# Dense products with no reader ahead of two waits of TensorE

## The chip, the cores and the metric

The kernel runs on one core of a Trainium2 chip. The metric is the device time of one execution in microseconds (us), lower is better. A run with the hardware profiler switched on gives the trace from which the rows below come.

## The reference, cut to what matters

2 x 2048 token ids out of 64 become rows of 256 numbers: 179 from an embedding table, 77 from a projected magnitude spectrum of the one-hot signal, interpolated between 33 frames. Then

```
h = tok(x)                                            # (2, 2048, 256)
h = h + local_attention(layernorm(h))                 # softmax over 5 neighbours
h = h + moe(layernorm(h))                             # 8 experts, top 2, capacity 1280
# moe: logits = x @ router_w + b; two best experts of each token, weights renormalised
#      h1 = gelu(rows of an expert @ w1[e] + b1[e]);  out = h1 @ w2[e] + b2[e]
```

## The kernel before, in words

A token's row is a mixture of 98 table rows (64 ids, 33 frames, one constant). The attention stage works on 8 groups (`NG`) of 512 tokens, each of 4 tiles of 128. All its products are of 32-bit operands. The order is written out by hand for each engine, with semaphores between the engines.

TensorE's order for one group is `attend(g)`: `mix(g)` (lines 1192 and 1194, probabilities times table coordinates), `scores(g + 1)` (line 1164, then transpositions at 1169 and 1171), `residual(g)` (lines 1205 and 1206, two products for each tile), `turn_probs(g + 1)` (lines 1182 and 1183: it waits for the probabilities and transposes them), `table_times_u(g + 2)` (line 1157), and `rank(c)` where a chunk of groups has been routed (lines 1218 to 1225). `turn_probs` waits for `probs_ready` from VectorE, and for `hc_ready`, ScalarE's copies of all four tiles of `residual`. Inside `residual` tile t waits for ScalarE's copy of tile t - 2.

ScalarE copies the score coordinates (533), the transposed tables (539), the exponentials (548), the turned probabilities (554), the mixture (589), the residual's results (600), and scales rows for the experts (567) and for the output (576). Its exponentials of group g + 1 stand between the copies of `residual(g)`. VectorE adds the mask to the scores (794), takes the maximum (798), normalises (804, 806), takes statistics (818), and runs the routing of a chunk as chains of small instructions (842 to 958), after which it makes the low halves of the rows (966). The chunks of routing are groups 0 and 1, 2 and 3, 4 and 5, 6, 7.

GpSimd sends the routed rows to device memory, one indirect DMA for each tile and each of the two choices (451). When the first choices of all chunks have been sent (`sent_low`), SyncE's queue loads the rows of the first half expert, transposed (421), and their meta data (423). TensorE then runs `layer1` (1261) and `layer2` (1275) on 16 half experts, products of 16-bit operands with 320 and 256 columns. GpSimd adds the results to the output by indirect DMA (474).

`bank[0]` holds scores of two of a group's four tiles until VectorE has added the mask (`masked`); `w1s[:, 0, 0, 0, :]` is written when the first weight pair has been made (`stage_free`).

Of the kernel before, what the change touches and what calls it, by code (L numbers as in the profile page):

```python
# [33 lines left out]
P = 128  # L34
# [32 lines left out]
CHUNKS = ((0, 2), (2, 2), (4, 2), (6, 1), (7, 1))  # L67
# [23 lines left out]
def wait(eng, sem, value):  # L91

    if isinstance(value, int) and value <= 0:
        return
    eng.wait_ge(sem, value)


def build(nc, ids_frames, ids_win, window, emb, proj_w, proj_b, wq, wk, wv, bqk, bv, wr, br,
          w1, b1, w2, b2, consts, frames_of, masks, out):
    with ExitStack() as ctx:  # L100
        def sb(name, shape, dt=F32):
            return ctx.enter_context(nc.sbuf_tensor(name, shape, dt))

        def sem(name):
            return ctx.enter_context(nc.semaphore(name))


        w1s = sb("w1s", [P, 2, E, 2, FF], F16)
# [97 lines left out]
        def route(dims, dt=F32):  # L206
# [40 lines left out]
        bank = [ctx.enter_context(nc.psum_tensor(f"bank{i}", [P, 512], F32)) for i in range(8)]  # L247
# [30 lines left out]
        u_ready, g_done, g_ready, s_done, masked, max_ready, nmax_ready = (sem(n) for n in (  # L278
            "u_ready", "g_done", "g_ready", "s_done", "masked", "max_ready", "nmax_ready"))
# [5 lines left out]
        hout_ready, scaled, pair_hi, stage_free = (sem(n) for n in (  # L285
            "hout_ready", "scaled", "pair_hi", "stage_free"))
# [10 lines left out]
        sent_low = [sem(f"sent_low{c}") for c in range(len(CHUNKS))]  # L297
# [9 lines left out]
        def chunk_tiles(c):  # L307
            first, n = CHUNKS[c]
            return range(TPG * first, TPG * (first + n))
# [742 lines left out]
        def _(pe):  # L1052
            mm = nc.tensor.matmul
# [27 lines left out]
            for b in range(B):  # L1081
                for kt in range(2):
                    last = mm(bank[5][0:KZ, b * KZ:(b + 1) * KZ], tcT[:, kt, b, :], tcT[:, kt, b, :],
                              start=(kt == 0), stop=(kt == 1))
# [23 lines left out]
            for b in range(B):  # L1108
                for kt in range(2):
                    mm(bank[5][0:KZ, b * H:(b + 1) * H], tcT[:, kt, b, :], wv_s[:, kt, :],  # L1110
                       start=(kt == 0), stop=False)
                last = mm(bank[5][0:KZ, b * H:(b + 1) * H], con[0:1, C_ROW97:C_ROW97 + KZ], bv_s[0:1, :],
                          start=False, stop=True)
# [4 lines left out]
            for b in range(B):  # L1118
                for j in range(2):
                    last = mm(bank[4][0:KZ, b * KZ:(b + 1) * KZ], qT[:, j, b, :], kT[:, j, b, :],  # L1120
                              start=(j == 0), stop=(j == 1))
# [23 lines left out]
            for n, src in enumerate((tcT, tvT)):  # L1145
                for b in range(B):
                    at_ = (n * B + b) * E
                    for kt in range(2):
                        last = mm(bank[3][0:KZ, at_:at_ + E], src[:, kt, b, :], wr_s[:, kt, :],
                                  start=(kt == 0), stop=(kt == 1))  # L1150
# [8 lines left out]
            def scores(g):  # L1159
# [8 lines left out]
                for t in range(TPG):  # L1168
# [2 lines left out]
                nc.tensor.transpose(bank[5][0:2 * WCTX, TPG * KZ:(TPG + 1) * KZ], u[:, GRP:WIN],  # L1171
                                    ident[0:KZ, 0:KZ]).then_inc(ut_done, 1)

            def turn_probs(g):

                pe.wait_ge(probs_ready, g + 1)
                if g == 0:
                    pe.wait_ge(tabs_ready, 2)
                wait(pe, prT_ready, 2 * g)
                wait(pe, hc_ready, TPG * g)  # L1180
                for t in range(TPG):
                    nc.tensor.transpose(bank[3][:, t * P:(t + 1) * P], pr[:, t, 0:P], ident)  # L1182
                    last = nc.tensor.transpose(bank[7][0:2 * WCTX, EXTRA + t * 32:EXTRA + (t + 1) * 32],
                                               pr[P - 32:P, t, P:KEYS], ident[P - 32:P, P - 32:P])
                last.then_inc(pt_done, 1)
# [23 lines left out]
            def rank(c):  # L1209

                tiles = chunk_tiles(c)
                n = len(tiles)
                first, groups = CHUNKS[c]
                pe.wait_ge(counts_ready, c + 1)
                pe.wait_ge(misc_ready, 5)
                pe.wait_ge(ut_ready, 2 * min(first + groups + 2, NG))
                cells = counts[:, tiles[0]:tiles[-1] + 1, :]
                mm(ranks[:, 0:n * E], tri_b[:, :], cells.rearrange("p t e -> p (t e)"), start=True, stop=False)
                if c:
                    mm(ranks[:, 0:n * E].rearrange("p (t e) -> p t e", e=E), ones_b[:, :],  # L1220
                       before_b[:, :].unsqueeze(1).to_broadcast([P, n, E]), start=False, stop=False)
                for t in range(n - 1):
                    mm(ranks[:, (t + 1) * E:n * E].rearrange("p (t e) -> p t e", e=E), ones_b[:, :],
                       cells[:, t:t + 1, :].to_broadcast([P, n - 1 - t, E]), start=False, stop=False)
                mm(ranks[:, 0:n * E].rearrange("p (t e) -> p t e", e=E), ones_b[0:1, :],
                   base_b[0:1, :].unsqueeze(1).to_broadcast([1, n, E]), start=False, stop=True).then_inc(ranks_done, 1)

            def attend(g):
                more, more2 = g + 1 < NG, g + 2 < NG
                mix(g)  # L1230
                if more:
                    for c in ended(g - 2):
                        pe.wait_ge(ranks_read, c + 1)
                    scores(g + 1)
                residual(g)
                if more:
                    turn_probs(g + 1)
                if more2:
                    table_times_u(g + 2)
                for c in ended(g - 1):  # L1240
                    rank(c)

            table_times_u(0)
            scores(0)
            turn_probs(0)
            table_times_u(1)
            for g in range(NG):
                attend(g)
            rank(len(CHUNKS) - 1)


            def layer1(k):
# [125 lines left out]
```

## Time and profile before

| | |
|---|---|
| three runs | 472.61 us median (471.72 to 472.97) |
| the profiled execution | 467.62 us |
| its span, first to last instruction | 465.6 us |
| mean granted TensorE clock | 0.859 |
| TensorE busy | 364.2 us (78%) |
| VectorE, ScalarE, GpSimd busy | 273.2, 219.0, 227.2 us |

The clock is given as a share of full speed: 1.00 is 2.4 GHz, 0.50 is 1.2 GHz, and a mean between them is a stretch that had both. PE is TensorE, PEld its loading of the stationary operand, DVE VectorE, ACT ScalarE, POOL GpSimd, SPq SyncE's queue. Attention runs from about 62 to 198 us, the hand-over to the experts from 198 to 238 us, the experts from 238 us on.

### The profile page before, as it was taken

The numbers are of one execution on the slowest core, as the hardware profiler recorded it, in microseconds if no ns is written. First come the engines' busy times: TensorE is split into PE (matmuls) and PEld (weight loads), VectorE is DVE, ScalarE is ACT, GpSimd is POOL, SyncE is SP. The second block draws the span as 40 slices with busy tenths as digits, with TensorE's granted clock in tenths as the row PEclk, the third lists the DMA queues.
The fourth block names the chain that finished last, engine by engine and source line by source line (L and its number), as shares of the span: only waits on it lengthen the run. The fifth ranks groups of instructions, "written<-read, shape, count | busy, mean of one in ns | idle before, by whom it ended". The sixth has DMA issues, their size and how long they took to land.

```text
span 465.6 us, 7030 instructions
## 1 busy us (share of the span) xinstructions
PE 364.2 (78%) x2541; PEld 274.3 (59%) x2541; DVE 273.2 (59%) x753; ACT 219.0 (47%) x472; POOL 227.2 (49%) x167
## 2 busy tenths in 40 slices
PE   3079966998995995900059999999999999999950
PEld 3067443766762763600037778888877778888740
DVE  5824663448548458875009766666777766666630
ACT  3217876565562563541036554444555554444520
POOL 1035753300345346447740666555565676646682
PEclk9999975799596597565569999999999999999995
DMA  7839719866324223253288687778877787735463
GB/s 187 214 99 377 251 37 384 369 255 223 94 91 134 81 82 122 89 182 115 101 196 153 79 109 112 104 106 107 103 113 81 95 106 108 109 40 56 55 68 34
DMA packets 83462, 63.10 MB, mean 136 GB/s; under 512 B 56176, under 2 KB 77041, under 8 KB 82050
## 3 DMA queue, kind: packets, MB, share of 16 engines
q1 hardware_dynamic: 68836, 43.25, 34.1%
q0 software_dynamic: 14592, 19.41, 25.7%
q8 instruction: 20, 0.33, 0.3%
q14 instruction: 14, 0.11, 0.1%
HBM read 16.09 MB, written 36.06 MB: 112 GB/s over the span
## 4 chain that ended last, share of the span: by engine, by line
PE 61%; DVE 12%; POOL 9%; issue 6%; DMA 6%; ACT 2%; SPq 1%; ACTq 0%; DVEq 0%; POOLq 0%
PE bank L1261 20%; PE bank L1275 17%; POOL out L474 6%; PE bank L1192 3%; POOL slot_rows L451 3%; PE bank L1157 3%; PE bank L1205 3%; PE bank L1194 2%; PE bank L1182 2%; PE bank L1206 2%; DMA out<-reg_h,meta 2%; PE bank L1164 2%; DMA con<-consts 2%; PE bank L1069 1%; ACT reg_a L548 1%
## 5 line engine op out<-in xcount | busy, mean ns | idle before, releaser
L474 POOL DMA_INDIRECT out<-reg_h,meta x80 | 128.0, 1600 | 90.1 <-DVE reg_h L1038 57.8
L1261 PE MATMUL bank<-reg_z,w1s 128*128 128x320 f16 x768 | 108.8, 303 | 26.0 <-DMA meta<-slot_rows 26.0
L1275 PE MATMUL bank<-w2s,reg_h 128*128 128x256 f16 x960 | 107.3, 273 | 2.0 <-DVE reg_h L1030 2.0
L1261 PEld LDWEIGHTS bank<-reg_z,w1s 128*128 128x128 f16 x768 | 75.7, 99 | 55.9 <-issue 26.1
L451 POOL DMA_INDIRECT slot_rows<-reg_z,slots x64 | 64.2, 1003 | 89.5 <-DVE reg_z L966 73.0
L1275 PEld LDWEIGHTS bank<-w2s,reg_h 128*128 128x128 f16 x960 | 93.7, 98 | 14.1 <-DVE reg_h L1030 2.3
L641 ACT ACTIVATE reg_a<-bank,b1s 128x320 f32<-128x320 f32 x128 | 67.4, 527 | 37.4 <-PE bank L1261 33.1
L1038 DVE SCALAR_TENSOR_TENSOR reg_h<-reg_p,meta,reg_h 128x256 f32<-128x256 f32 x80 | 38.8, 485 | 55.8 <-ACT reg_h L653 49.3
L653 ACT ACTIVATE reg_h<-bank,meta 128x256 f32<-128x256 f32 x80 | 37.9, 474 | 68.2 <-PE bank L1275 64.9
L1028 DVE TENSOR_SCALAR reg_h<-reg_a 128x320 f16<-128x320 f32 x128 | 49.9, 390 | 33.5 <-DMA slot_rows<-reg_z,slots 27.1
L1030 DVE SCALAR_TENSOR_TENSOR reg_h<-reg_a,reg_h 128x320 f16<-128x320 f32 x128 | 63.0, 492 | 4.4
L1205 PE MATMUL bank<-ta,reg_a 98*128 98x265 f32 x64 | 25.7, 491 | 8.2 <-issue 6.0
L1206 PE MATMUL bank<-tb,reg_a 98*128 98x265 f32 x64 | 24.0, 464 | 0.0
L438 POOL TENSOR_TENSOR w1s<-reg_h,w1s 128x1024 f16<-128x1024 f32 x6 | 12.8, 2130 | 21.6 <-ACT w1s L492 21.6
L1205 PEld LDWEIGHTS bank<-ta,reg_a 98*128 98x128 f32 x64 | 14.0, 241 | 13.2 <-issue 7.3
L1182 PE MATMUL bank<-con,reg_a 128*128 128x128 f32 x32 | 12.3, 386 | 10.9 <-DVE reg_a L806 9.2
L794 DVE TENSOR_TENSOR reg_a<-bank,reg_a 128x264 f32<-128x264 f32 x16 | 6.2, 427 | 22.6 <-PE bank L1164 22.6
L1192 PE MATMUL bank<-reg_a 128*98 128x128 f32 x64 | 19.1, 390 | 0.4 <-ACT reg_a L555 0.4
L966 DVE SCALAR_TENSOR_TENSOR reg_z<-reg_h,r,reg_z 128x256 f16<-128x256 f32 x32 | 13.6, 480 | 8.4 <-ACT reg_z L567 8.2
L600 ACT ACTIVATE reg_h<-bank 128x265 f32<-128x265 f32 x32 | 12.3, 383 | 12.1 <-PE bank L1206 7.2
L1206 PEld LDWEIGHTS bank<-tb,reg_a 98*128 98x128 f32 x64 | 15.1, 236 | 3.7
L1069 PE MATMUL bank<-reg_a,reg_h 128*33 128x77 f32 (+1 forms) x68 | 6.7, 270 | 13.1 <-DVE reg_h L714 13.1
(167 smaller groups left out, 426.5 us busy)
## 6 DMA issues: line engine op xcount, KB each, us to landing
slot_rows<-reg_z SPq DMA_DIRECT2D x8, 1360.0 KB, 9.5
reg_h<-w SPq DMA_DIRECT2D x12, 512.0 KB, 8.6
out<-reg_p SPq DMA_DIRECT2D x8, 512.0 KB
reg_w<-w SPq DMA_DIRECT2D x4, 512.0 KB, 10.2
reg_a<-inv_rows SPq DMA_DIRECT2D x8, 193.5 KB
out<-reg_z SPq DMA_DIRECT2D x1, 1280.0 KB, 13.0
out<-reg_h,meta POOLq DMA_INDIRECT x80
reg_a<-masks SPq DMA_DIRECT2D x1, 1056.0 KB, 12.9
```

The source lines that it names most:

```text
L451: nc.gpsimd.indirect_dma_start(out=slot_rows, out_offset=bass.IndirectOffsetOnAxis(ap=slots[:, side, n:n + 1], axis=0), in_=x2w[:, n % RIN ...
L474: nc.gpsimd.indirect_dma_start(out=out.rearrange("t p c -> (t p) c"), out_offset=bass.IndirectOffsetOnAxis(ap=meta[:, k, s, 0:1], axis=0), ...
L641: nc.scalar.activation(gel[:, n % GB, :], bank[n % 4][:, 0:CH], ACT.Gelu, bias=b1s[:, e, f:f + 1], scale=1.0 / (X_SCALE * W_SCALE)).then_i ...
L653: nc.scalar.activation(y[:, k % 2, s, :], bank[4 + n % 4][:, 0:H], ACT.Copy, scale=metaf[:, k, s, 1 + e:2 + e]).then_inc(y_scaled, 1)
L1028: ts(hT[:, k % 2, 0, f, cols], gel[:, n % GB, :], X_SCALE, None, ALU.mult).then_inc(hi_ready, 1)
L1030: stt(hT[:, k % 2, 1, f, cols], gel[:, n % GB, :], X_SCALE, hT[:, k % 2, 0, f, cols], ALU.mult, ALU.subtract).then_inc(lo_ready, 1)
L1038: stt(y[:, k % 2, s, :], b2s[:, e, :], metaf[:, k, s, 1 + e:2 + e], y[:, k % 2, s, :], ALU.mult, ALU.add).then_inc(y_ready, 1)
L1192: mm(bank[2][0:KZ, t * P:(t + 1) * P], ut[:, t, :], prT[:, t * P:(t + 1) * P], start=True, stop=False)
L1205: mm(bank[6 + t % 2][:, 0:OW], zq[:, t * P:(t + 1) * P], ta_b, start=True, stop=False)
L1206: mm(bank[6 + t % 2][:, 0:OW], yT[:, t * P:(t + 1) * P], tb_b, start=False, stop=True).then_inc(o_done, 1)
L1261: last = mm(bank[n % 4][:, 0:CH], w1s[:, wp, e, kt, f * P:(f + 1) * P], xT[:, k % XB, 2 * xp + kt, c * CH:(c + 1) * CH], start=(kt == 0 an ...
L1275: last = mm(bank[4 + n % 4][:, 0:H], hT[:, k % 2, hp, f, s * P:(s + 1) * P], w2s[:, wp, e, f, :], start=(f == 0 and hp == 0 and wp == 0), ...
```

## The change: what it does

A helper `keep_busy(n)` issues n products of 128x128 by 128x512 16-bit operands, weights in both places, into `bank[0]`. Each starts its own sum and nobody reads the bank before it is written again. Four of them stand in `turn_probs(g)` ahead of the wait for probabilities, for g from 1 to 7; they wait until group g's scores have been read out of the bank, and for the weights. Twelve stand between the last `rank` and the first `layer1`, behind a wait for the last chunk's first-choice rows, the event that also lets SyncE load the first half expert.

```diff
+            def keep_busy(n):
+
+                for i in range(n):
+                    mm(bank[0][:, :], w1s[:, 0, 0, 0, 0:P], w1s[:, 0, 0, 0, :], start=True, stop=True)
+
             def turn_probs(g):
 
+                if g:
+                    pe.wait_ge(masked, 2 * (g + 1))
+                    pe.wait_ge(stage_free, 1)
+                    keep_busy(4)
                 pe.wait_ge(probs_ready, g + 1)
...
             rank(len(CHUNKS) - 1)
+            pe.wait_ge(sent_low[len(CHUNKS) - 1], 16 * len(chunk_tiles(len(CHUNKS) - 1)))
+            keep_busy(12)
```

## Rows read from the trace of the kernel before

**Rows 1.** The span in 40 slices: TensorE's busy tenths and granted clock.

```profile
PE   3079966998995995900059999999999999999950
PEclk9999975799596597565569999999999999999995
```

**Rows 2.** The chain that ended last, shares of the span by engine.

```profile
PE 61%; DVE 12%; POOL 9%; issue 6%; DMA 6%; ACT 2%; SPq 1%; ACTq 0%; DVEq 0%; POOLq 0%
```

**Rows 3.** Busy time, clock (the 0.5 to 1.0), DMA: turning to turning, groups 1 to 7.

```profile
91.17:102.15 10.98, 10.41 (x55) 7.28 (x56) 4.74 (x14) 7.14 (x22) 0.00 (x0) 1.00 0.52 184
102.15:114.49 12.34, 10.49 (x55) 7.29 (x55) 11.06 (x50) 7.28 (x23) 0.00 (x0) 1.00 0.82 299
114.49:131.85 17.36, 16.79 (x64) 11.91 (x65) 8.85 (x28) 9.52 (x28) 4.18 (x4) 0.61 0.23 74
131.85:149.83 17.98, 12.31 (x56) 7.84 (x56) 12.61 (x54) 7.96 (x25) 11.62 (x12) 0.81 0.41 135
149.83:166.88 17.05, 16.48 (x66) 11.43 (x66) 8.62 (x28) 9.41 (x28) 4.16 (x4) 0.60 0.18 63
166.88:183.26 16.38, 11.80 (x55) 7.73 (x56) 12.42 (x53) 7.96 (x25) 11.15 (x12) 0.91 0.35 125
183.26:198.50 15.24, 14.19 (x56) 9.97 (x56) 11.42 (x56) 6.80 (x18) 5.69 (x6) 0.53 0.23 83
```

**Rows 4.** The same view of two stretches at the low clock.

```profile
115.70:129.20 13.50, 13.50 (x51) 9.76 (x51) 6.55 (x22) 7.70 (x21) 4.18 (x4) 0.50 0.30 96
181.00:197.30 16.30, 14.68 (x51) 9.78 (x51) 13.58 (x65) 7.28 (x20) 6.37 (x7) 0.50 0.23 84
```

**Rows 5.** TensorE in order of time: start, length, and in brackets the idle before.

```profile
97.68 0.64 PE L1205 MATMUL bank<-ta,reg_a 98*128 98x265 f32 x2
...
102.15 0.32 PE L1182 MATMUL bank<-con,reg_a 128*128 128x128 f32 x1 [0.57 <-DVE reg_a L806]
...
114.49 0.33 PE L1182 MATMUL bank<-con,reg_a 128*128 128x128 f32 x1 [1.85 <-DVE reg_a L806]
...
142.36 0.81 PE L1205 MATMUL bank<-ta,reg_a 98*128 98x265 f32 x2 [2.03 <-issue]
...
145.51 1.25 PE L1205 MATMUL bank<-ta,reg_a 98*128 98x265 f32 x2 [1.45 <-ACT reg_h L600]
...
149.83 0.47 PE L1182 MATMUL bank<-con,reg_a 128*128 128x128 f32 x1 [2.19 <-DVE reg_a L806]
...
180.56 1.25 PE L1205 MATMUL bank<-ta,reg_a 98*128 98x265 f32 x2 [1.98 <-issue]
...
183.26 0.45 PE L1182 MATMUL bank<-con,reg_a 128*128 128x128 f32 x1 [0.57 <-issue]
```

**Rows 6.** ScalarE in order of time, in rounds 3 and 7.

```profile
118.75 2.49 ACT L567 ACTIVATE reg_z<-reg_h,r 128x256 f16<-128x256 f32 x6
121.14 1.69 ACT L576 ACTIVATE reg_p<-reg_h 128x256 f32<-128x256 f32 x4
...
193.15 0.23 ACT L583 ACTIVATE reg_r<-reg_r 128x32 f32<-128x32 f32 x1 [1.45 <-DVE reg_r L883]
```

**Rows 7.** VectorE in order of time, in rounds 4 and 7.

```profile
142.55 0.77 DVE L794 TENSOR_TENSOR reg_a<-bank,reg_a 128x264 f32<-128x264 f32 x2
...
199.26 0.88 DVE L966 SCALAR_TENSOR_TENSOR reg_z<-reg_h,r,reg_z 128x256 f16<-128x256 f32 x2 [2.21 <-ACT reg_z L567]
```

**Rows 8.** GpSimd in order of time, behind the attention stage.

```profile
207.61 1.35 POOL L451 DMA_INDIRECT slot_rows<-reg_z,slots  x1 [5.35 <-DVE reg_z L966]
```

**Rows 9.** The chain in order of time, at the first experts: start, length, what.

```profile
227.98 2.46 DMA slot_rows<-reg_z,slots
...
233.56 3.89 DMA meta<-slot_rows
237.58 15.27 PE bank L1261 x96
...
259.40 6.52 PE bank L1261 x48
```

## The prediction

> **What bounds the kernel now.** I read the span in slices first [rows 1]: from slice 21 on TensorE is busy without a break at full clock, so the experts stay as they are; the granted clock is down in the attention slices and around the hand-over. The chain of waits puts 61% on TensorE [rows 2]. The question is thus where TensorE works at the low clock while it sets the pace. For that I cut attention at the start of each turning of probabilities, rounds 1 to 7 [rows 3]. Rounds 1 and 2 run at 1.00 and take 10.98 and 12.34 us. Rounds 3 and 5 run at 0.61 and 0.60, with TensorE busy 16.8 of 17.4 and 16.5 of 17.1 us: TensorE sets the pace there, slowly. Rounds 4 and 6 have it busy for 12.3 of 18.0 and 11.8 of 16.4 us; another engine rules. In round 4 VectorE adds the mask at 142.55 us with no idle time before it, so it is late from its own routing chain, and TensorE's breaks of 2.03, 1.45 and 2.19 us follow from that [rows 5, 7]. Round 7 is at 0.53, and in it TensorE works 14.2 of 15.2 us.
>
> The low stretch of round 3 is 13.5 us at 0.50 (1.2 GHz), with no break in the work [rows 4]. Just before it TensorE sat idle for 1.85 us ahead of the third turning [rows 5]. The falls in rounds 4 and 6 come with breaks of about 2 us inside `residual`; no filler stands there. In both the clock was low again when the next odd round began.
>
> **What leads from attention to the end.** Behind attention GpSimd sat idle for 5.35 us until 207.61 us, then sent rows without a stop [rows 8]; it started when VectorE had the rows, which hangs on the last residual copies. So what round 7's end gains or loses goes through to the experts, up to those 5.35 us for a gain that VectorE's or GpSimd's own work does not share.
>
> **One filler's price.** The trace has no 512-column product. 48 products of 320 columns take 6.52 us at full clock, 0.136 us each or 0.424 ns a column [rows 9]: 512 columns take 0.217 us, four 0.87 us. In the first 96, which took 15.27 us, 2.23 us went to the low clock against 13.04. At half the clock a product costs twice: four take 1.74 us, twelve 5.2 us. Bounds: if their issue were as slow as two instructions of the turning (0.32 us one by one at full clock, [rows 5]), four would take 1.3 us; if the engine takes them while it would wait anyway, nothing. I take 0.87 and 1.74.
>
> **Where four fillers cost.** A turning starts 0.57 us after the residual's last product, even where the probabilities are there, since it waits for ScalarE's last copy. That is so in the rows of turnings 2 and 7 and three more times [rows 5]. There, warm fillers cost 0.87 - 0.57 = 0.3 us: turnings 1, 2, 4 and 6, 1.2 us. At turning 7 the clock is low (1.2 GHz from 181 us, [rows 4]), so 1.74 - 0.57 = 1.15 us (bounds 0.3 and 1.2). Ahead of turnings 3 and 5 TensorE waits 1.85 and 2.19 us [rows 5]; fillers of 0.87 and 1.74 fit in: nothing. The added waits for `masked` and the weights are long past there: masked scores are what the exponentials are made from. Sum of costs 2.35 us.
>
> **Round 3, the gain.** With 0.87 us of dense products in it the 1.85 us break becomes 0.98 us, less than half of the breaks at which the clock fell. I take it that the clock stays at full here. What is the round then worth? Round 1 took 10.98 us, all warm. Round 3 has two things more: a `rank`, and on ScalarE six scalings of rows and four output copies, 4.08 us from 118.75 to 122.83, ahead of the copy of the mixture [rows 6]. In round 1 the residual started 97.68 - 91.17 = 6.5 us after the turning [rows 5]. In a warm round 3, ScalarE would be through the coordinates' copy some 3.1 us after the turning, with its 4.08 us at 7.2 and with the mixture (0.6 us) at about 7.75: the residual starts 1.2 us later than in round 1. That covers the rank, too. 10.98 + 1.2 = 12.2 us against 17.36 us [rows 3]: a gain of 5.2 us (bounds: 0 if the clock falls all the same; 6.4 if ScalarE's copies cost nothing). The next round starts as much earlier, and all of its order with it, VectorE's routing included, since that starts from this round's copies.
>
> **Rounds 4 to 7.** Round 4 keeps its length of 18 us, bound by VectorE; its breaks inside `residual` have no filler, so I expect the clock low at turning 5 as before, round 5 the same as now, and round 6 and 7 the same but for the costs above.
>
> **The twelve.** They may start when the last chunk's first rows are down, about 230.4 us (227.98 + 2.46), and the first half expert's rows land at 237.5 us [rows 9]. Twelve at the low clock take 5.2 us and end at 235.6, ahead of the landing: no cost. If the clock rises on the way they end sooner. Either way about 2 us of idle time follow, as long as the breaks at which the clock fell in attention [rows 5]. So of the 2.23 us at most I take 1.0 us (bounds 0 and 2.2).
>
> **Sum.** + 2.35 - 5.2 - 1.0 = - 3.85 us. The profiled execution of before is 467.62 us (span 465.6), which gives 463.8. The timed runs have a median of 472.61, 5.0 us above the profiled one, so the forecast for them is 468.8 us.
>
> The moment at which the clock turns is the weak point. Worked out of the mean clocks, rounds 3, 5 and 7 spent 13.5, 13.6 and 14.3 us at the low one (twice the missing share by the length, [rows 3]), and in each it rose only near the round's end. The Trainium skill ("TensorE: Matmul & The Clock Gate", Part 1, section "What's actually happening") says that the number of products run cold at a start varies between runs of one kernel. By that rule the 5.2 and 1.0 us are not a property of the kernel alone, and the before of another execution might not fall at turning 3; one profiled execution can't show it.
>
> **Rivals.**
> - The fillers also lift the clock ahead of turning 5 or 7. There the residual's last tile is followed by 1.74 us of dense work, in all 3.9 us with hardly a break from 145.51 or 180.56 us [rows 5]. For it: the clock has risen in `residual` before, the densest stretch. Against: it took many us of work each time. At turning 5 a warm round would be some 12.2 us long, as worked out above, against 17.05: 4.8 us more gained. At turning 7 VectorE's routing limits it: ScalarE waits until 193.15 us for VectorE's logits [rows 6], and only the residual's tail shortens; since VectorE's rows at 199.26 us have 2.21 us of idle time in front [rows 7], 2.2 us is all that can be given, and the 1.15 us cost goes too: 3.35 us. Times: 464.0 (turning 5), 465.4 (turning 7), 460.6 (both).
> - Slower: the clock falls in round 3 all the same. Place: turning 3. 0.98 us of idle time are left there, and the turning waits on its transpositions behind it; that is enough for the fall. Price: the costs stand, 2.35 us, the gain is 0, and where the twelve bring nothing either (they end 2 us early) the time is 475.0 us. It decides if the granted clock is 0.5 within 2 us of turning 3.
> - The timed runs of before do not have the fall of round 3, as in the rule above: nothing to save there, - 3.85 + 5.2 = + 1.35, 474.0 us. Against it: their times lie within 1.25 us, less than 5.2, so they'd have to share another pattern; and they are slower than the profiled one, not faster.
> - Round 3's gain is given back: VectorE, GpSimd's sending or the transfers hold round 4 at its old place. Half of the gain gone makes 471.4 us. Against it: VectorE idles 2.6 us more than once in round 3, busy 8.85 of 17.36 us [rows 3].
>
> **How the numbers follow.** Forecast 0.30; further rises 0.36 (only at 7 0.17, only at 5 0.12, both 0.07); falls all the same 0.17; before without the fall 0.07; given back 0.10. Two runs of this kernel can be told apart from about 0.3%, 1.4 us. Faster by more: the forecast and the rises and 0.06 of the rest, 0.72. Slower by more: most of the fourth and some of the fifth case, 0.15. Same: 0.13. The range leaves out the double rise and most of the slower case with no help from the twelve: 461.0 to 474.5 us.
>
> **What would show it.** In the changed trace: the clock at 1.00 from turning 3 to the break in round 4's residual, and round 3 about 12 us long (right), or 17 (wrong). Fillers of 0.217 us each warm, 0.43 cold. Turnings 1, 2, 4, 6 0.3 us later behind the residual. Round 4 still 18 us, round 5 at 0.6. A first half expert of 13 to 15.3 us. The prediction is wrong if round 3 keeps its length, if round 4 grows by what round 3 gave, or if the clock is at 1.00 in round 5 or 7.

## The result, and the profile after

The changed kernel takes 466.75 us (median of 4 runs, 464.33 to 467.81) against 472.17 us before (4 runs, 471.15 to 472.97): a ratio of 0.9879, 95% interval 0.9835 to 0.9924, some 5.4 us faster. The forecast was 468.8 us in a range of 461.0 to 474.5. The profiled execution took 464.33 us with a span of 462.5 us and a mean clock of 0.876 (before: 467.62, 465.6 and 0.859). Where a kernel had a run more than 1.5% above its fastest, that run is not in its ratio; this is one run each of three kernels below (468.74, 534.70 and 471.95 us).

The same cut as in [rows 3], turning to turning, for the changed kernel; after the busy times come clock, DMA share and GB/s. The last two rows are the hand-over and the first 96 expert products:

```profile
91.24:102.32 11.08, 11.08 (x60) 7.68 (x59) 4.74 (x13) 7.14 (x22) 0.00 (x0) 1.00 0.53 191
102.32:114.61 12.29, 11.31 (x60) 7.55 (x59) 10.95 (x50) 7.28 (x23) 0.00 (x0) 1.00 0.81 296
114.61:126.92 12.31, 11.70 (x69) 8.26 (x69) 8.76 (x28) 9.18 (x28) 4.19 (x4) 1.00 0.28 84
126.92:146.43 19.51, 13.46 (x61) 8.18 (x59) 12.73 (x54) 8.08 (x25) 11.66 (x12) 0.82 0.38 137
146.43:163.54 17.11, 17.11 (x69) 11.87 (x70) 8.75 (x28) 9.41 (x28) 4.17 (x4) 0.61 0.19 64
163.54:181.41 17.87, 13.46 (x61) 8.21 (x60) 12.94 (x55) 7.96 (x25) 11.66 (x12) 0.87 0.34 124
181.41:195.90 14.49, 13.55 (x56) 9.45 (x56) 10.91 (x54) 6.93 (x18) 5.68 (x6) 0.57 0.23 81
195.90:234.80 38.90, 5.01 (x19) 1.88 (x20) 15.38 (x68) 6.02 (x16) 25.70 (x26) 0.56 0.47 150
234.80:249.67 14.87, 14.87 (x98) 10.24 (x99) 9.12 (x26) 8.97 (x16) 1.36 (x2) 0.89 0.83 156
```

The third row is the gain: round 3 went from 17.36 us at 0.61 to 12.31 us at 1.00. Rows 4 and 6 give part of it back: 19.51 for 17.98 us and 17.87 for 16.38 us. Together that is 3.0 us of the 5.05. Round 5 is as it was, round 7 is 0.9 us shorter (turning to the start of the last `rank` in both traces, 14.09 for 14.98 us) and the first 96 products 0.4 us.

TensorE in order of time, changed kernel, around turnings 3, 5 and 7 and at the hand-over (L1177 are the fillers, L1191 the turning):

```profile
112.60 1.03 PE L1177 MATMUL bank<-w1s 128*128 128x512 f16 x4
114.61 0.33 PE L1191 MATMUL bank<-con,reg_a 128*128 128x128 f32 x1 [0.99 <-DVE reg_a L806]
...
142.48 1.91 PE L1177 MATMUL bank<-w1s 128*128 128x512 f16 x4
146.43 0.47 PE L1191 MATMUL bank<-con,reg_a 128*128 128x128 f32 x1 [2.04 <-DVE reg_a L806]
...
179.11 1.91 PE L1177 MATMUL bank<-w1s 128*128 128x512 f16 x4
181.41 0.45 PE L1191 MATMUL bank<-con,reg_a 128*128 128x128 f32 x1 [0.38 <-ACT reg_h L600]
...
227.79 4.58 PE L1177 MATMUL bank<-w1s 128*128 128x512 f16 x12 [18.98 <-DMA slot_rows<-reg_z,slots]
234.80 14.87 PE L1272 MATMUL bank<-reg_z,w1s 128*128 128x320 f16 x96 [2.43 <-issue]
```

The idle time ahead of turning 3 went from 1.85 to 0.99 us [rows 5] and the clock stayed. Ahead of turning 5 it is still 2.04 us, behind fillers of 1.91 us. That is what is odd in the trace: round 4 had a wait of 2.19 us for them to fit in [rows 5], and should not have grown. ScalarE shows why, in round 4 of the changed kernel:

```profile
140.13 0.37 ACT L600 ACTIVATE reg_h<-bank 128x265 f32<-128x265 f32 x1
142.13 0.39 ACT L600 ACTIVATE reg_h<-bank 128x265 f32<-128x265 f32 x1 [0.86 <-remote]
145.71 0.39 ACT L600 ACTIVATE reg_h<-bank 128x265 f32<-128x265 f32 x1 [3.18 <-remote]
```

The residual's last tile was done at 142.7 us and its copy starts 3.0 us later, with no releaser that the profile knows ("remote"). I call this a hold-up below. The experiments had to say whether the fillers cause it.

### The profile page after: what moved, and what is told of

Read it like the earlier page. It is cut to its first block, busy times and chain, and to the rows that moved or that the text cites. A ratio compares the mean times of both kernels' runs of the same rounds, so it can differ in the third digit from the quotient of the medians.

```text
span 462.5 us, 7117 instructions
## 1 busy us (share of the span) xinstructions
PE 368.0 (80%) x2581; PEld 274.0 (59%) x2581; DVE 273.7 (59%) x753; ACT 218.6 (47%) x472; POOL 227.1 (49%) x167
## 4 chain that ended last, share of the span: by engine, by line
PE 61%; DVE 16%; POOL 8%; issue 6%; DMA 4%; ACT 3%; another core or an unknown queue 1%; SPq 0%; DVEq 0%; ACTq 0%; POOLq 0%
PE bank L1272 22%; PE bank L1286 19%; POOL out L474 4%; POOL slot_rows L451 3%; PE bank L1157 2%; PE bank L1214 2%; PE bank L1164 2%; PE bank L1191 2%; PE bank L1177 2%; PE bank L1201 2%; DMA con<-consts 2%; PE bank L1215 2%; PE bank L1069 1%; DVE reg_z L966 1%; PE bank L1203 1%
## 5 line engine op out<-in xcount | busy, mean ns | idle before, releaser
L1214 PE MATMUL bank<-ta,reg_a 98*128 98x265 f32 x64 | 24.3, 467 | 9.3 <-issue 6.0
L1177 PE MATMUL bank<-w1s 128*128 128x512 f16 x40 | 13.5, 484 | 19.0 <-DMA slot_rows<-reg_z,slots 19.0
L438 POOL TENSOR_TENSOR w1s<-reg_h,w1s 128x1024 f16<-128x1024 f32 x6 | 12.8, 2130 | 21.5 <-ACT w1s L492 21.5
L1215 PE MATMUL bank<-tb,reg_a 98*128 98x265 f32 x64 | 22.2, 433 | 0.0
L1214 PEld LDWEIGHTS bank<-ta,reg_a 98*128 98x128 f32 x64 | 12.9, 224 | 14.0 <-issue 7.3
L1177 PEld LDWEIGHTS bank<-w1s 128*128 128x128 f16 x40 | 4.7, 120 | 25.5 <-DMA slot_rows<-reg_z,slots 19.1
L600 ACT ACTIVATE reg_h<-bank 128x265 f32<-128x265 f32 x32 | 12.3, 383 | 15.8 <-remote 6.7
L1201 PE MATMUL bank<-reg_a 128*98 128x128 f32 x64 | 17.9, 369 | 0.2 <-ACT reg_a L555 0.2
L1191 PE MATMUL bank<-con,reg_a 128*128 128x128 f32 x32 | 12.0, 376 | 7.4 <-DVE reg_a L806 7.0
```

The source lines that it names most:

```text
L1177: mm(bank[0][:, :], w1s[:, 0, 0, 0, 0:P], w1s[:, 0, 0, 0, :], start=True, stop=True)
L1214: mm(bank[6 + t % 2][:, 0:OW], zq[:, t * P:(t + 1) * P], ta_b, start=True, stop=False)
L1215: mm(bank[6 + t % 2][:, 0:OW], yT[:, t * P:(t + 1) * P], tb_b, start=False, stop=True).then_inc(o_done, 1)
```

## The experiments

All ran in groups, each group on one chip with its own runs of the kernel before: 467.0 us for the first four kernels, 466.8 for the next four, 471.0 for the next three, 469.5 for the last. The times that the expectations name assume a before of 472.2 us (first group) or 467 us (the others), so ratios are compared, not times.

**Parts of the change.** Four kernels: the attention fillers without the twelve; the twelve alone; fillers ahead of turning 3 alone; ahead of all but 3.

```diff
-                if g:                 # keep_busy(4) ahead of every turning from 1
+                if g == 3:            # third only;  "if g and g != 3:" all but the third
-            pe.wait_ge(sent_low[len(CHUNKS) - 1], 16 * len(chunk_tiles(len(CHUNKS) - 1)))
-            keep_busy(12)
```

> The change without the twelve. Theory (the gain is round 3's clock): 0.4 to 1.5 us slower than the whole change, whose trace had the first 96 expert products in 14.87 us against 15.27 before, so 467.2 to 468.3 us; round 3 12.3 us long at clock 1.00. Rival (the hand-over's clock brings much of the gain): 469 us or more.

Measured: 461.53 us, ratio 0.9905 (0.9867 to 0.9943), 5.5 us under its before: as a ratio within the theory's range.

> Only the twelve, no fillers in attention. Theory: 0 to 1.5 us faster than before (the time of before 472.2 us, so 470.7 to 472.2), the first 96 products 14 to 15.3 us; round 3 still 17 us at 0.61. Rival (timed executions gain mainly at the hand-over): 468 to 470 us.

Measured: 466.68 us, ratio 0.9992 (0.9971 to 1.0013). That is the theory's range. The twelve bring at most 1.4 us, and nothing that these runs can tell.

> Four fillers ahead of turning 3 alone. Theory: the whole gain of round 3 (5.2 us) and none of the other costs; round 4 keeps its 18.0 us instead of the 19.5 us of the changed kernel and round 6 its 16.4 instead of 17.9. So 466 to 467.5 us, faster than the full set of attention fillers by 1 to 3 us. Rival A (all fillers keep the clock up together; the one at 3 alone does not hold it): 471 us or more. Rival B (rounds 4 and 6 grew because they began at other times, not by their fillers): rounds 4 and 6 19.5 and 17.9 us here too, and the time that of the full set.

Measured: 462.25 us, ratio 0.9898 (0.9864 to 0.9931), but six runs from 460.27 to 468.74 (that last one has the clock of before, 0.856). The theory had it 1 to 3 us faster than the full set of attention fillers; it was not faster. The profiled one is among the slower ones (465.47), and there the clock fell in round 3 after all, at the same 0.99 us of idle time: 

```profile
115.28:131.11 15.83, 15.26 (x64) 10.87 (x65) 8.71 (x28) 9.41 (x28) 4.18 (x4) 0.68 0.26 81
131.11:147.83 16.72, 11.80 (x55) 7.71 (x55) 12.76 (x54) 7.96 (x25) 11.48 (x12) 0.90 0.41 136
```

Rounds 4 and 6 took 16.72 and 16.39 us, so rival B (they grew because they began at other times) did not come true here.

> Fillers ahead of turnings 1, 2, 4, 5, 6, 7, not 3. Theory: only costs, 0.1 us each where warm (1, 2, 4, 6) and about 1.5 us each for the two at the low clock (5 and 7): 472.2 + 0.4 + 3.0, 473.5 to 476 us, round 3 at 0.6. Rival (the others lift the clock on the way): 472 us or less, with a clock over 0.61 in round 5 or over 0.53 in round 7.

Measured: 461.80 us, ratio 0.991 (0.9883 to 0.9937). My theory of this run fell: without the filler at 3 the kernel gains as much. The trace of this kernel says where, in rounds 3 to 7:

```profile
114.03:131.42 17.39, 17.39 (x69) 12.30 (x69) 8.99 (x29) 9.52 (x28) 4.18 (x4) 0.61 0.21 74
131.42:148.69 17.27, 14.12 (x60) 8.81 (x59) 13.09 (x56) 7.96 (x25) 11.60 (x12) 0.81 0.40 132
148.69:161.04 12.35, 11.77 (x71) 8.16 (x69) 8.05 (x26) 9.18 (x28) 4.15 (x4) 0.99 0.26 91
161.04:178.32 17.28, 13.25 (x60) 8.41 (x59) 13.24 (x56) 7.96 (x25) 11.63 (x12) 0.84 0.35 127
178.32:191.79 13.47, 11.84 (x57) 8.27 (x55) 10.41 (x53) 6.87 (x18) 5.40 (x6) 0.70 0.26 92
```

Round 3 is slow as before and round 5 is 12.35 us at 0.99: the four fillers behind the residual's last tile lifted a clock that had fallen. That was my rival "further rises". In time order, first this kernel and then the attention fillers with all seven places (one transposition of a turning takes 0.33 us at the full clock, 0.47 at the low one):

```profile
146.98 1.91 PE L1177 MATMUL bank<-w1s 128*128 128x512 f16 x4
149.11 0.33 PE L1191 MATMUL bank<-con,reg_a 128*128 128x128 f32 x1
...
143.26 1.91 PE L1177 MATMUL bank<-w1s 128*128 128x512 f16 x4
145.46 0.47 PE L1191 MATMUL bank<-con,reg_a 128*128 128x128 f32 x1
```

In both the residual's last tile and the fillers make 3.6 us of work without a break ahead of turning 5 (from 145.06 and 141.33 us), and only in the first did the clock rise: round 3 was 12.31 us in that second trace, but round 5 18.42 us at 0.56. So the lift, too, comes in some executions and not in others. The parts also do not add: the set without the third and the third alone gain some 4 to 5 us each, both together (the attention fillers) hardly more.

**Where the others work.** Only the warm places 1, 2, 4, 6, and only 5 and 7:

```diff
-                if g:
+                if g in (1, 2, 4, 6):        # and:  if g in (5, 7):
```

> Four fillers ahead of turnings 1, 2, 4 and 6 alone, where the clock was at full and TensorE had at most 0.57 us of idle time. Theory (these cost 0.1 us each and lift nothing): within 1 us of before (467.0 us on the last chip), ratio 1.000 to 1.002. Rival (any filler helps the clock, wherever it stands): ratio 0.993 or less.

Measured: 466.91 us, ratio 1.0008 (0.9992 to 1.0024). They do nothing that these runs can tell, as the theory had it; round 3 of the trace is 17.38 us at 0.61.

> Four fillers ahead of turnings 5 and 7 alone, where the clock had fallen before. Theory (what the set without the third gained comes from these two, which bring the clock back behind the residual's last tile): 461 to 463 us where before is 467.0, round 5 near 12.4 us or round 7 near 13.4 us in the profile, against 17.1 and 15.4. Rival (the two at the low clock only cost): 468 to 470 us, rounds 5 and 7 as before and rounds 4 and 6 longer by 0.6 to 0.9 us.

Measured: 461.07 us, ratio 0.9892 (0.9864 to 0.9919). Two fillers' places alone bring as much as all, in the theory's range. Round 5 of its trace, and round 7:

```profile
148.26:160.54 12.28, 11.12 (x67) 7.64 (x65) 7.93 (x27) 9.19 (x28) 4.15 (x4) 0.99 0.25 88
...
177.26:190.93 13.67, 11.52 (x56) 8.34 (x56) 11.77 (x57) 6.76 (x18) 5.45 (x6) 0.75 0.26 92
```

**In the breaks themselves.** Eight fillers ahead of each of the two late tiles of the residual in rounds 4 and 6, where the trace of before has the breaks of 2 us [rows 5]. The same kernel has eight ahead of turnings 5 and 7, four ahead of 3, and none elsewhere:

```diff
+                    if g in (4, 6) and t > 1:
+                        keep_busy(8, 2)              # into bank[2], free there
                     wait(pe, hc_ready, TPG * g + t - 1)
```

> Fillers where the trace shows the breaks: eight ahead of each of the two late tiles of the residual in rounds 4 and 6 (into the bank of the mixture, free by then), eight ahead of turnings 5 and 7, four ahead of 3; none ahead of 1, 2, 4, 6, none at the hand-over. Theory (the breaks in rounds 4 and 6 make rounds 5 and 7 slow): rounds 3 and 5 12.3 us each at 1.00, round 7 about 13 us, rounds 4 and 6 unchanged at 16.7 to 17 and 16.4; 5.0 + 4.8 + 2.2 us less than before, 455 to 457 us where before is 467.0, and the runs closer together. Rival (VectorE's routing takes over and holds the rounds, so that a full clock brings little more than the change): 460 to 462 us.

Measured: 457.37 us, ratio 0.9804 (0.9785 to 0.9822), 9.4 us under its before and the five runs within 3.4 us. The clock is at 1.00 through rounds 4, 5 and 6:

```profile
115.45:132.96 17.51, 16.94 (x65) 12.07 (x65) 9.14 (x29) 9.64 (x28) 4.18 (x4) 0.61 0.21 74
132.96:149.66 16.70, 15.99 (x79) 9.52 (x80) 12.33 (x53) 7.97 (x25) 11.50 (x12) 1.00 0.41 137
149.66:161.84 12.18, 11.03 (x65) 7.78 (x66) 8.53 (x28) 9.19 (x28) 4.27 (x5) 1.00 0.26 90
161.84:178.25 16.41, 15.85 (x80) 9.68 (x80) 12.45 (x53) 7.96 (x25) 11.19 (x12) 1.00 0.37 133
178.25:191.02 12.77, 11.55 (x57) 8.27 (x55) 11.31 (x56) 6.87 (x18) 4.69 (x5) 0.73 0.25 89
```

Rounds 4 and 6 keep their 16.7 and 16.4 us with eight products in each break: VectorE rules there, and the fillers are free. Rounds 5 and 7 are 12.2 and 12.8 us. The clock of 1.00 through round 4 is the work of the fillers inside the residual, since the eight at turning 5 come behind it; what those in the residual and those at the turnings bring in rounds 5 and 7 was not run apart. Round 3 fell again with four fillers ahead of it; of the four traces with exactly four there (the change, its attention part, the third alone, this one) two held the clock. The time is just outside the theory's 455 to 457 us, which had counted on round 3.

**The hand-over.** 22 products, so that TensorE works until the rows land:

> Only the hand-over, with 22 products instead of 12, so that TensorE is busy until the first rows land. Theory (VectorE waits for the last second-choice rows before it may write, and so holds the first expert whatever the clock): the first 96 products 14.0 to 14.3 us, no shorter than with twelve, and the time 0.5 to 1.2 us under before, 465.8 to 466.5 where before is 467.0. Rival (the clock alone bounds the first expert): 13.0 to 13.3 us and 464.5 to 465.

Measured: 465.64 us, ratio 0.9973 (0.9958 to 0.9988). TensorE in order of time:

```profile
229.63 7.46 PE L1177 MATMUL bank<-w1s 128*128 128x512 f16 x22 [18.65 <-DMA slot_rows<-reg_z,slots]
236.93 6.68 PE L1272 MATMUL bank<-reg_z,w1s 128*128 128x320 f16 x48
243.95 6.68 PE L1272 MATMUL bank<-reg_z,w1s 128*128 128x320 f16 x48 [0.34 <-ACT reg_a L641]
250.47 5.73 PE L1286 MATMUL bank<-w2s,reg_h 128*128 128x256 f16 x51
```

From the first product to the second layer 13.54 us, between theory and rival (before: 15.11 us): 48 products at full clock, then a stop of 0.34 us, since VectorE had not begun. Its first work on an expert, from the same trace:

```profile
242.33 0.33 DVE L1028 TENSOR_SCALAR reg_h<-reg_a 128x320 f16<-128x320 f32 x1 [26.55 <-DMA slot_rows<-reg_z,slots]
```

It waits for the last second-choice rows. In the kernel with the twelve alone that stop was 0.86 us and the stretch 14.06 us. In the trace of before:

```profile
237.58 15.27 PE L1261 MATMUL bank<-reg_z,w1s 128*128 128x320 f16 x96 [26.04 <-DMA meta<-slot_rows]
252.69 6.71 PE L1275 MATMUL bank<-w2s,reg_h 128*128 128x256 f16 x60
...
243.22 0.33 DVE L1028 TENSOR_SCALAR reg_h<-reg_a 128x320 f16<-128x320 f32 x1 [27.12 <-DMA slot_rows<-reg_z,slots]
```

From this first work of VectorE to the second layer it is 8.14 us with the 22 and 9.47 us before, so that at most 1.3 us are to be had. The runs are 1.2 us under their before, not the 2.23 us of the clock's own price.

Then three kernels in the group with 471.0 us before: the 22 products without VectorE's wait (its edit is below), every break filled, and eight ahead of turning 3 alone.

```diff
-                if k == 0:
-                    dve.wait_ge(sent_high[last], 16 * len(chunk_tiles(last)))
```

> Only the hand-over's 22 products, and VectorE no longer waits for the last second-choice rows before its first work on an expert (it writes another region). Theory (that wait holds the first expert once the clock is up): the first 96 products 13.0 to 13.3 us, 464.3 to 465 where before is 467, about 1 us under the 22 with the wait. Rival (VectorE's early work slows GpSimd's sending of rows, or the wait only hides another): the first 96 still 14 us or the second half expert's start later, 465.5 us or more.

Measured: 472.85 us, ratio 1.0051 (1.0028 to 1.0074), slower. In its trace ScalarE's table load comes at 245.78 us, 4.4 us after TensorE's first expert product at 241.42; before, it was 1.84 us (239.42 behind 237.58). VectorE then stood behind ScalarE, so the run can't tell what the wait costs.

> Every break of the attention stage filled in: the fillers of the kernel with eight inside the residual, but eight ahead of turning 3 too (four let the clock fall there in two of four traces), three ahead of the residual of rounds 3, 5 and 7 while it waits for the copy of the mixture, and 22 at the hand-over. Theory: rounds 3 and 5 12.3 us, round 7 12.8 us, all at 1.00, and the first expert at 14.1 to 14.8; 452 to 453.5 us where before is 467, 4 to 5 us under the 457.4 of the kernel with fillers in the residual. Rival (a longer stretch of fillers delays the copies and takes the gain back): 457 us or more.

Measured: 469.33 us, ratio 0.9939 (0.9909 to 0.9968): the theory failed, and the time is on the rival's side. The mean clock was 0.895, as high as in the 457 us kernel. Rounds 3, 4 and 6 ran at 1.00, but rounds 4 and 6 took 19.67 and 19.65 us with hold-ups of 4.4 us, and ScalarE's table load came 5.3 us behind the first expert product (242.01, 236.76).

> Eight fillers ahead of turning 3 alone, where four left 0.99 us of idle time. Theory (what counts is the break that is left): the clock holds in every run, 461 to 462 us with all runs within 1.5 us of the median, where four gave 460.3 to 468.7. Rival (whether the clock falls does not hang on that break): runs as spread as with four, some at 467 us.

Measured: 466.73 us, ratio 0.9906 (0.9875 to 0.9936), 4.2 us under its before; round 3 in the trace 12.18 us at 1.00. The runs' clocks lie from 0.866 to 0.873 (with four: 0.856 to 0.876), their times from 464.2 to 468.4, which is no wider than their before (467.5 to 472.5) but misses the theory's 1.5 us. The traces say more. Where nothing stood ahead of turning 3 and some 1.85 us of idle time were left, the clock fell in all seven; with four products and 0.99 us left, in two of four; with eight and no idle time that the rows list, in none of three (this one, every break filled, and the last kernel below). But rounds 4 and 6 were long here, too, with no filler anywhere near them:

```profile
114.40:126.58 12.18, 11.00 (x64) 7.73 (x65) 8.61 (x28) 9.19 (x28) 4.20 (x4) 1.00 0.32 86
126.58:145.86 19.28, 11.81 (x55) 7.74 (x56) 13.29 (x55) 7.98 (x25) 11.65 (x12) 0.83 0.41 138
...
163.09:182.36 19.27, 12.75 (x55) 8.21 (x56) 12.99 (x55) 7.98 (x25) 11.68 (x12) 0.77 0.32 116
```

And in the kernel of the hand-over without VectorE's wait, whose attention stage is that of the kernel before, ScalarE shows the same hold-up as in the changed kernel:

```profile
145.11 0.37 ACT L600 ACTIVATE reg_h<-bank 128x265 f32<-128x265 f32 x1
147.03 0.39 ACT L600 ACTIVATE reg_h<-bank 128x265 f32<-128x265 f32 x1 [0.78 <-remote]
150.61 0.39 ACT L600 ACTIVATE reg_h<-bank 128x265 f32<-128x265 f32 x1 [3.19 <-remote]
```

So the fillers of the attention stage are not needed for it. It stands in all traces of the last two groups and in none of the eight of the first two, whatever the kernel.

**The best version.** The kernel with fillers in the residual and eight ahead of turning 3:

```diff
-                    keep_busy(8 if g in (5, 7) else 4)
+                    keep_busy(8)                     # g in (3, 5, 7)
```

> The kernel with eight fillers ahead of each late tile of the residual in rounds 4 and 6 and ahead of turnings 5 and 7, now with eight instead of four ahead of turning 3 as well; nothing at the hand-over. Theory (each break filled keeps the clock up, and a clock kept at turning 3 is worth another 5 us): rounds 3 and 5 12.2 us, ratio to before 0.968 to 0.975, 452 to 455.5 us where before is 467. Rival (the gains do not add: with round 3 warm the breaks of rounds 4 and 6 come at other places and the clock falls there): ratio 0.980 or more, as with four.

Measured: 466.69 us against 469.54, ratio 0.9929 (0.9907 to 0.995), in the rival's range, though not for the rival's reason:

```profile
115.27:127.45 12.18, 11.00 (x65) 7.75 (x65) 8.61 (x28) 9.19 (x28) 4.20 (x4) 1.00 0.31 87
127.45:147.13 19.68, 16.01 (x80) 9.54 (x80) 12.85 (x54) 7.98 (x25) 11.64 (x12) 1.00 0.38 135
147.13:164.26 17.13, 16.56 (x65) 11.55 (x66) 8.67 (x28) 9.43 (x28) 4.16 (x4) 0.60 0.19 64
```

The clock holds through rounds 3 and 4; then ScalarE's hold-up leaves TensorE idle for 3.10 us ahead of turning 5, fillers spent, and round 5 is slow. With the hold-up this kernel gains 2.9 us; its near twin gained 9.4 us where there was none. The two ran on different chips, so what eight instead of four ahead of turning 3 do without a hold-up was not measured. A version that is best on both was not found. No trace has both round 3 and round 5 at the full clock.

## Why the prediction was right, point by point

- **What bounds it, and round 3.** The step that carried the forecast held in size: 5.05 us gained (17.36 to 12.31) for 5.2, the round 12.3 us long for 12.2, its residual 7.75 us behind the turning (122.36 for 114.61) for 7.7. The mechanism was seen apart in the kernel with eight ahead of turning 3 alone: 12.18 us at 1.00 and a ratio of 0.9906. What I took as a fact of the kernel, that 0.98 us of idle time keeps the clock, is a matter of chance: held in two of four traces, so that the trace of the change showed it was luck. I had also argued that 0.98 us is less than half of the breaks at which the clock fell; of the 1.85 us at this place it is more than half.
- **Fillers where it is warm.** Forecast 0.3 us each, measured 0.1 us: round 1 took 11.08 for 10.98 us, round 2 none more. I had subtracted the 0.57 us wait from the end of the last product as the profile draws it; the next products start before that end. In the changed kernel the filler starts at 90.37 us and the turning 0.87 us later. 1.2 us became about 0.4: the four warm places alone gave 1.0008, which is 0.4 us with an interval that includes nothing.
- **Fillers where it is cold.** Ahead of turning 7 1.15 us forecast; round 6 took 17.26 and 17.28 us with them and 16.35 to 16.39 us without, in the first two groups: 0.9 us. (With fillers ahead of 5 and 7 alone it took 16.72 us; there the four ran at the full clock, drawn 1.03 us long.) Ahead of turning 5 I forecast nothing; round 4 took 17.27 to 17.30 us with and 16.67 to 16.72 without: 0.6 us. The wait of 2.19 us that was to hide them [rows 5] held some 1.2 us in which VectorE stood still in that execution; in the traces without such a stop the wait is 0.90 us.
- **Rounds 5 to 7.** Round 5 as before (17.11 us), right for the profiled execution. But a rise ahead of turning 5 or 7, my rival at 0.36, is what two of the fillers do: alone they gave 0.9892. I priced it at 4.8 us for turning 5 (measured 17.05 to 12.3, 4.8 us) and at 3.35 us for turning 7, of which 2.2 us were round 7's and 1.15 us the cold cost gone. To the same event, round 7 took 13.2 to 13.7 us for 15.4, 1.7 to 2.2 us less, but the cold cost of 0.9 us stayed in two of the three traces. With the breaks of rounds 4 and 6 filled round 7 was 12.8 us, more than the 2.2 us that I had called the most. Which of the changed kernel's timed runs had it can't be told from their clocks (0.876 to 0.881).
- **The twelve.** 1.0 us forecast; 0.4 us in the trace of the change, and the twelve alone 0.9992, in which 1.0 is not excluded. The bound of 2.2 us was too high: by the trace of the kernel with 22, VectorE's wait for the second-choice rows caps the gain near 1.3 us. The run without that wait could not test this.
- **The sum.** - 3.85 us forecast, - 3.3 us in the profiled executions (464.33 for 467.62), - 5.4 us in the timed ones. Part of the nearness is luck: rounds 4 and 6 grew by 3.0 us, of which the fillers explain 1.5 (0.6 and 0.9), against 1.15 forecast; that was made up by warm places cheaper than forecast and by round 7. And the timed gain is 2.1 us more than the profiled one, by a share that no trace splits into rounds. Why the profiled execution of before stood 5 us under its timed runs is not shown. It had a short hold-up only, and the groups without hold-ups have a before of 467.0 and 466.8 us, those with them 471.0 and 469.5. In the kernel with the same attention stage and long hold-ups rounds 4 and 6 took 19.46 and 18.52 us, together 3.6 us more than in [rows 3]; that would make up most of it, but I have no trace of before itself with them.

On the rule that I cited (the Trainium skill, "TensorE: Matmul & The Clock Gate", Part 1, "What's actually happening"): the runs agree that it varies between executions whether the clock turns at one place. One kernel, with four products ahead of turning 3, gave clocks from 0.856 to 0.876 and times 8.5 us apart, while the kernel before stayed between 0.855 and 0.862 in 22 of 23 runs of that group. The doubt that I drew from it, that another execution of before might not fall at turning 3, did not come true in any trace: the clock fell there in all seven whose break was not filled.

Of my signs, round 3 of 12 us, round 5 at 0.6 and a first half expert of 13 to 15.3 us came (12.31, 0.61, 14.87). Round 4 was to be 18 us and was 19.5, and the warm turnings were to be 0.3 us later and were 0.1.

## What to carry to other kernels

Cut a stage by its rounds, and read clock and length of each: where TensorE rules at the low clock, look for the break just ahead of it. Products that nobody reads are free in breaks where another engine is late; they should fill the break (eight for 2 us), not shorten it, for a shortened break keeps the clock only in some runs. What a warm clock is worth is read from the next wait behind it: 5 us in round 5, some 2 us in round 7, 1.2 us of 2.2 at the hand-over.

## What the runs showed that I had not expected

In some groups, each on a chip of its own, ScalarE stands still at one point of rounds 4 and 6 with its inputs ready: ahead of the residual's last copies, 2.7 to 4.4 us. VectorE stops there too, by 0.5 to 1.9 us at a time. A hold-up with a "remote" releaser stands in five traces (the changed kernel and the four kernels of the last two groups) and in none of the eight of the first two groups. It comes in kernels with and without fillers there. The two kernels with 22 products at the hand-over in these groups also had ScalarE start on the first expert 4.4 and 5.3 us behind the first product, the other two 1.84 us and the changed kernel, with twelve, 1.77 us, so that there the 22 may have to do with it. The same 22 on another chip did nothing of the kind (1.06 us). What holds the engines was not found. GpSimd's row transfers run at that point, but they do so in the traces without a hold-up as well.

A second thing is open: gains of rounds 3 and 5 did not come together in any trace, though each came alone. In three of the five traces with a fast round 3 a hold-up left 2 to 3.1 us of idle time at turning 5, fillers spent; the fourth had no filler there and 3.45 us; in the fifth, without a hold-up, four fillers did not lift the clock. Whether that last is chance, or the shift of 5 us puts the later breaks in a worse place, was not told apart.
